# A value product issued one core step after its exponential, where it was issued two steps after

## The chip, the cores and the metric

The kernel runs on one core of a Trainium2 chip, as one launch. The metric is the device time of that launch in microseconds. Engines are named as in the profile: PE (TensorE matmuls), PEld (its weight loads), DVE (VectorE), ACT (ScalarE), POOL (GpSimd), SP (SyncE, which here only issues DMAs).

## What is computed

The input is a batch of 8 sequences of 1024 tokens with 256 channels, in float32. Each goes through six residual blocks, each on a layer norm: a gated feed-forward, a chunked linear attention, the feed-forward again, a routed low-rank expert block, a causal softmax attention, and the expert block again. The change is in the softmax attention:

```python
# 16 heads of 16 channels, scale = 16 ** -0.5; q and k carry a rotary embedding
scores = jnp.einsum('bhqd,bhkd->bhqk', q, k) * scale
scores = jnp.where(causal, -jnp.inf, scores)
attn = jax.nn.softmax(scores, axis=-1)
out = jnp.einsum('bhqk,bhkd->bhqd', attn, v)
```

## The kernel before, in words

**Three streams.** A front (feed-forward, linear attention, feed-forward, expert block, projections to q, k and v), a core (the softmax attention) and a tail (output projection and last expert block) run at the same time for different sequences. Each engine executes one fixed list of instructions, written by `weave` (L446). It counts ticks; in four of five ticks there is one core step `t`, and it calls the engine's core function three times, with `part` 0, 1 and 2. Between these calls come the pieces of the front for the first 512 tokens (after part 0), of the front for the last 512 tokens (after part 1) and of the tail (after part 2). No engine leaves its order.

**The core.** A group `g` is four heads of one sequence, 32 groups in all. A first pass computes scores (`score`, L730, with a mask added by a small matmul L733) whose row maxima DVE takes (`reduce_max`, L1083); the banks of these scores are a ring of two, shared with two kinds of transposes (L783, L789), so each score waits until DVE has read the one two places back. The maxima go back through DRAM as extra rows of the stacked q (`stq`), so that the second pass gets scores with the maximum already subtracted.

**The second pass** is cut into units `u`, 24 for a group and 768 in all: a half `c` of the queries, a block `kb` of 128 keys, and a pair `hp` of heads; even units hold heads 0 and 1 of the group and odd ones heads 2 and 3. Core step `t` has `u = t - SX`. In it

- PE computes the transposed scores of unit `u + 1` (`tscore`, L747), a matmul for each of two heads, into banks 0 and 1. The matmul of head `j` waits until ACT has read that bank for unit `u`.
- ACT takes the exponentials of unit `u` (L1283), one instruction a head, into `pexp`, a ring of `NPX = 4` units in SBUF. Before it writes slot `u % 4` it waits for `pv_done`, which counts value products of pairs.
- POOL sets the part over the diagonal to zero in units of the causal diagonal (`affine_select`, L1431; 16 of 24 units), one step after ACT in its own list.
- PE multiplies values and exponentials of a pair of units, four heads at once (`values`, L766; eight matmul records), into bank 2. It waits for the exponentials of the odd unit, for POOL's selects, and at the first key block of a half for ACT's copy of bank 2 (`ypv`, L1289) from the half before.
- When a half is complete ACT copies bank 2, PE transposes the copy (L783) and DVE divides by the row sums (L1070, L1074).

SP loads stacked q and k of a later group when the transposed scores of an earlier one are done (L1483), and rows of v when value products have let go of them (L1492).

The wait of ACT that matters below is this one:

```python
if u >= NPX:
    nc.scalar.wait_ge(s["pv_done"], (u - NPX) // 2 + 1)
```

For even `u` it asks for the pair whose last unit is `u - 3`; for odd `u` for the pair whose last unit is `u - 4`, which is the same pair. In the list of PE the kernel before issues the pair ending in unit `u - 2` at odd `u`, in part 1, so the pair that ends in `u - 3` comes right behind the transposed scores of the even unit `u`.

Of the kernel before, what the change touches and what calls it, by code (L numbers as in the profile page):

```python
# [18 lines left out]
NB = B  # L19
# [36 lines left out]
def macaron(nc, a, out):  # L56
    ctx = ExitStack()
    with ctx:
# [105 lines left out]
        def ps(i, n=1):  # L164
            return bank[i // 2][:, (i % 2) * CH:(i % 2) * CH + n * CH]
# [192 lines left out]
        NU = NTU * NG  # L358
# [23 lines left out]
        def width(c, kb):  # L382
            return CH - max(0, kb - 4 * c) * P
# [18 lines left out]
        if True:  # L402

            with nc.Block() as block:
# [22 lines left out]
                def r_take(*key):  # L427
                    n = len(rtab)
                    rtab[key] = n
                    if n >= 2:  # L430
                        nc.tensor.wait_ge(s["r_used"], n - 1)
                    return ps(3 + n % 2)
# [290 lines left out]
                def score(g, i):  # L723

                    h, qb, k0, k1 = sunits[i]
                    b_ = slot(g, h // 2)
                    nc.tensor.wait_ge(stack_in[b_], 16 * ND * loads(g, h // 2))
                    bk = r_take("s", g, i)
                    diag = k1 == P * (qb + 1)
                    last = mm(bk[:, 0:k1 - k0], stq[b_][:, h % 2, qb * P:(qb + 1) * P], stk[b_][:, h % 2, k0:k1],  # L730
                              start=True, stop=not diag)
                    if diag:
                        last = mm(bk[:, k1 - k0 - P:k1 - k0], identb[:], maskneg[:], start=False, stop=True)  # L733
                    last.then_inc(s["r_full"], 1)

                def tscore(u):

                    g, i = divmod(u, NTU)
                    c, kb, hp = tunits[i]
                    if i == 0:  # L740
                        nc.tensor.wait_ge(max_in[g % 2], 64 * (g // 2 + 1))
                    n = width(c, kb)
                    b_ = slot(g, hp)
                    for j in range(2):
                        if u >= 1:
                            nc.tensor.wait_ge(s["exp_done"], 2 * u + j - 1)
                        mm(ps(j)[:, 0:n], stk[b_][:, j, kb * P:(kb + 1) * P],  # L747
                                  stq[b_][:, j, (c + 1) * CH - n:(c + 1) * CH], start=True, stop=True).then_inc(
                                      s["t_ps"], 1)

                def values(u):

                    g, i = divmod(u, NTU)
                    c, kb, _ = tunits[i]
                    yu = NC * g + c
                    n = width(c, kb)
                    if g % NG == 0 and kb % 4 == 0:
                        nc.tensor.wait_ge(s["v_in"], 32 * (g // NG) + 16 * (kb // 4 + 1))
                    nc.tensor.wait_ge(s["exp_done"], 2 * u + 2)
                    if i in DIAG:  # L760
                        nc.tensor.wait_ge(s["causal"], len(DIAG) * g + DIAG.index(i) + 1)
                    if kb == 0 and yu >= 1:
                        nc.tensor.wait_ge(s["ypv_done"], yu)
                    for j in range(G):
                        at = VP * (G * (g % NG) + j)
                        last = mm(ps(2)[HP * j:HP * (j + 1), CH - n:CH], vsm[:, kb, at:at + HP], pexp[:, (u - 1 + j // 2) % NPX, j % 2, 0:n],  # L766
                                  start=kb == 0, stop=kb == 4 * c + 3, tile_position=(0, HP * j))
                    last.then_inc(s["pv_done"], 1)

                def core_pe(t, part):  # L770
                    u = t - SX
                    if part == 0 and 0 <= u + 1 < NU * NB:
                        tscore(u + 1)
                    if part == 1 and u % 2 and 3 <= u < NU * NB + 2:
                        values(u - 2)
                    if (t, part) in score_at:
                        score(*score_at[t, part])
                    if part == 2 and t in y_tr_at:
                        g, c = y_tr_at[t]
                        nc.tensor.wait_ge(s["ypv_done"], NC * g + c + 1)  # L780
                        bk = r_take("y", g, c)
                        for k in range(4):
                            last = nc.tensor.transpose(bk[:, k * P:(k + 1) * P], ypv[:, c, k * P:(k + 1) * P], ident[:])  # L783
                        last.then_inc(s["r_full"], 1)
                    if part == 2 and t in max_tr_at:
                        g = max_tr_at[t]
                        nc.tensor.wait_ge(s["mx_comb"], g + 1)
                        bk = r_take("m", g)
                        nc.tensor.transpose(bk[0:G * NT, 0:P], mxa[:, g % 2], ident[:]).then_inc(s["r_full"], 1)  # L789

                @block.tensor
                def _(pe):
                    weave(core_pe, front_pe, tail_pe)
# [782 lines left out]
```

## Time and profile before

| | |
|---|---|
| Median of three runs | 3236.56 us (3227.16 to 3240.71) |
| The profiled execution | 3248.06 us, span of the core 3246.3 us |
| PE busy | 2891.0 us, 89% of the span |
| DVE busy | 1852.1 us, 57% |
| ACT busy | 1215.9 us, 37% |
| POOL busy | 746.2 us, 23% |
| Granted TensorE clock over the span | 0.922 |
| First transposed score to the last value product | from 391.8 us to 3175.6 us |

The profile is of one execution. Busy time is the union of an engine's instructions; idle time before an instruction is put down to the engine and line whose semaphore ended it. Waits under 0.15 us are left out of the views of waits. The granted clock is 1.00 at 2.4 GHz and 0.5 at 1.2 GHz. A difference of less than about half a per cent can't be told from the spread of the runs.

### The profile page before, as it was taken

Reading aid. Unit: us, or ns where it says so; the run is one execution under the profiler, and the core shown is the slowest. Engines: PE = TensorE matmul, PEld = TensorE weight load, DVE = VectorE, ACT = ScalarE, POOL = GpSimd, SP = SyncE. Lnnn points to the kernel's source line nnn. Section 1 sums busy time; section 2 is a strip of 40 time slices with the busy share of each in tenths; the row PEclk is TensorE's granted clock in tenths of the full one; section 3 lists DMA queues with packets and bytes.
Section 4 is the critical chain, followed back from the end, with each engine's and each line's share of the span. In section 5 each row is a group of like instructions: output and inputs, shape, how many; then the busy total and the mean of one; then the engine's idle time right before and its main releaser. Section 6 shows DMA issues by size and latency. Waiting matters only on the chain.

```text
span 3246.3 us, 47003 instructions
## 1 busy us (share of the span) xinstructions
PE 2891.0 (89%) x16398; PEld 1811.0 (56%) x16398; DVE 1852.1 (57%) x4515; ACT 1215.9 (37%) x2706; POOL 746.2 (23%) x1276
## 2 busy tenths in 40 slices
PE   3885899899999998999999999999999999989987
PEld 2653565456656665556656566466555566555534
DVE  6443656655666556665566556565566655665532
ACT  1321244344334343443334343343434333343341
POOL 1321222222222222223222222222322222221110
PEclk7886899999999999999999999999999989999986
DMA  1024104311232204311333113322134113233101
GB/s 54 1 59 105 21 16 95 94 27 37 55 109 57 58 16 102 106 39 30 63 83 89 36 38 61 110 57 51 26 92 115 30 30 63 70 89 98 44 21 41
DMA packets 137424, 194.06 MB, mean 60 GB/s; under 512 B 49439, under 2 KB 111214, under 8 KB 127854
## 3 DMA queue, kind: packets, MB, share of 16 engines
q1 hardware_dynamic: 137198, 191.07, 23.9%
q8 instruction: 139, 2.28, 0.3%
q14 instruction: 87, 0.71, 0.1%
HBM read 122.34 MB, written 67.63 MB: 59 GB/s over the span
## 4 chain that ended last, share of the span: by engine, by line
PE 65%; DVE 12%; DMA 7%; ACT 4%; issue 3%; SPq 1%; POOL 1%; DVEq 0%; ACTq 0%; POOLq 0%
PE bank L747 9%; PE bank L730 8%; PE bank L766 8%; DMA stk<-k_halves 6%; PE bank L565 4%; PE bank L658 4%; PE bank L505 3%; PE bank L514 3%; PE bank L672 3%; PE bank L545 3%; ACT pexp L1283 3%; PE bank L496 2%; PE bank L659 2%; DVE mxa L1083 2%; PE bank L475 2%
## 5 line engine op out<-in xcount | busy, mean ns | idle before, releaser
L1283 ACT ACTIVATE pexp<-bank 128x512 f32<-128x512 f32 (+3 forms) x1536 | 675.1, 496 | 934.2 <-PE bank L766 748.2
L1083 DVE TENSOR_REDUCE mxa<-bank 128x1 f32<-128x512 f32 (+3 forms) x1024 | 595.3, 587 | 506.9 <-PE bank L733 296.9
L730 PE MATMUL bank<-stk,stq 128*128 128x512 f32 (+3 forms) x1536 | 604.0, 415 | 148.2 <-DVE mxa L1083 53.2
L747 PE MATMUL bank<-stq,stk 128*128 128x512 f32 (+3 forms) x1536 | 592.3, 444 | 73.9 <-ACT pexp L1283 66.5
L730 PEld LDWEIGHTS bank<-stk,stq 128*128 128x128 f32 x1536 | 300.6, 198 | 466.8 <-issue 408.3
L1431 POOL TENSOR_SCALAR_AFFINE_SELECT pexp<-pexp 128x256 f32<-128x256 f32 x512 | 217.1, 428 | 911.5 <-ACT pexp L1283 911.4
L747 PEld LDWEIGHTS bank<-stq,stk 128*128 128x128 f32 x1536 | 281.9, 198 | 253.8 <-ACT pexp L1283 181.5
L766 PE MATMUL bank<-pexp,vsm 128*32 128x512 f32 (+3 forms) x3072 | 345.1, 523 | 0.0
L1083 DVE TENSOR_REDUCE mxb<-bank 128x1 f32<-128x128 f32 (+3 forms) x512 | 248.0, 484 | 167.5 <-PE bank L733 165.2
L733 PE MATMUL bank<-maskneg,identb 128*128 128x128 bf16 x1024 | 243.4, 238 | 0.0
L1349 POOL TENSOR_SCALAR_AFFINE_SELECT arena<-arena 128x512 f32<-128x512 f32 x128 | 78.4, 636 | 438.9 <-ACT arena L1187 438.9
L565 PE MATMUL bank<-arena 32*128 32x256 f32 x1024 | 159.2, 431 | 14.8 <-DVE arena L893 11.1
L733 PEld LDWEIGHTS bank<-maskneg,identb 128*128 128x128 bf16 x1024 | 102.2, 100 | 123.6 <-issue 78.3
L475 PE MATMUL bank<-ident,arena 128*128 128x128 f32 x768 | 119.9, 307 | 38.9 <-DVE arena L810 38.7
L496 PE MATMUL bank<-arena,wk 128*128 128x256 f32 x512 | 144.4, 433 | 8.3 <-ACT arena L1187 4.6
L1300 POOL TENSOR_SCALAR varep<-mv 128x4 f32<-128x4 f32 x96 | 22.6, 235 | 542.6 <-DVE mv L804 541.8
L1104 ACT COPY xnT<-bank 128x512 f32<-128x512 f32 x160 | 89.3, 609 | 144.8 <-PE bank L475 144.2
L505 PE MATMUL bank<-wr,arena 128*128 128x256 f32 x512 | 132.8, 406 | 1.0
L1405 POOL TENSOR_TENSOR arena<-arena 128x1024 f32<-128x1024 f32 x32 | 75.9, 2372 | 246.7 <-DVE arena L1008 246.7
L893 DVE TENSOR_TENSOR arena<-bank,mask 128x512 f32<-128x512 f32 x128 | 82.3, 685 | 87.9 <-PE bank L565 87.9
L475 PEld LDWEIGHTS bank<-ident,arena 128*128 128x128 f32 x768 | 101.8, 163 | 48.4 <-DVE arena L810 41.6
L514 PE MATMUL bank<-wv,arena 128*128 128x256 f32 x512 | 122.0, 382 | 3.3 <-ACT arena L1191 3.2
(185 smaller groups left out, 4146.8 us busy)
## 6 DMA issues: line engine op xcount, KB each, us to landing
stq<-q_halves SPq DMA_DIRECT2D x128, 256.0 KB
arena<-rope_table SPq DMA_DIRECT2D x8, 2048.0 KB
q_halves<-arena SPq DMA_DIRECT2D x32, 512.0 KB, 2.9
k_halves<-arena SPq DMA_DIRECT2D x32, 512.0 KB, 2.8
stk<-k_halves SPq DMA_DIRECT2D x64, 256.0 KB
stk<-k_halves SPq DMA_DIRECT2D x128, 128.0 KB
v_rows<-arena SPq DMA_DIRECT2D x16, 544.0 KB, 4.1
vsm<-v_rows SPq DMA_DIRECT2D x16, 544.0 KB, 3.8
```

Source lines behind the costliest of these rows:

```text
L475: last = nc.tensor.transpose(bk[:, t * P:(t + 1) * P], src[:, t, k * P:(k + 1) * P], ident[:])
L496: last = mm(bk[:, m * D:(m + 1) * D], wk0[:, k, m * P:(m + 1) * P], xmA[:, h, k], start=k == 0, stop=k == KT - 1)
L505: last = mm(bk[:, i * D:(i + 1) * D], xmB[:, p, k, i * P:(i + 1) * P], wr0[:, k], start=k == 0, stop=k == KT - 1)
L514: last = mm(bk[:, i * D:(i + 1) * D], kact[:, p, k, i * P:(i + 1) * P], wv0[:, k], start=k == 0, stop=k == KT - 1)
L565: last = mm(bks[i][:, k * D:(k + 1) * D], khT[rows, k, j * P:(j + 1) * P], qbd[rows, j % 2, k], start=k == 0, stop=k == KT - 1, skip_group ...
L730: last = mm(bk[:, 0:k1 - k0], stq[b_][:, h % 2, qb * P:(qb + 1) * P], stk[b_][:, h % 2, k0:k1], start=True, stop=not diag)
L733: last = mm(bk[:, k1 - k0 - P:k1 - k0], identb[:], maskneg[:], start=False, stop=True)
L747: mm(ps(j)[:, 0:n], stk[b_][:, j, kb * P:(kb + 1) * P], stq[b_][:, j, (c + 1) * CH - n:(c + 1) * CH], start=True, stop=True).then_inc(s["t ...
L766: last = mm(ps(2)[HP * j:HP * (j + 1), CH - n:CH], vsm[:, kb, at:at + HP], pexp[:, (u - 1 + j // 2) % NPX, j % 2, 0:n], start=kb == 0, sto ...
L1083: nc.vector.reduce_max(dst, r_bank("s", g, i)[:, 0:k1 - k0], AX).then_inc(s["r_used"], 1)
L1283: nc.scalar.activation(pexp[:, u % NPX, j, 0:n], ps(j)[:, 0:n], ACT.Exp, scale=DK ** -0.5).then_inc(s["exp_done"], 1)
L1431: nc.gpsimd.affine_select(out=v, in_=v, compare_op=ALU.is_ge, fill=0.0, base=0, pattern=[[0, 2], [1, P]], channel_multiplier=-1).then_inc( ...
```

## The change

Value products are issued at even `u` in place of odd `u`, and of the pair that ends in `u - 1` in place of `u - 2`. Every value product moves one core step ahead in PE's list, still in part 1. Nothing else of any engine's list changes: the waits ask for the same counts, the ring has four slots as before, and the same instructions run with the same sizes.

```diff
@@ -771,8 +771,8 @@
                     u = t - SX
                     if part == 0 and 0 <= u + 1 < NU * NB:
                         tscore(u + 1)
-                    if part == 1 and u % 2 and 3 <= u < NU * NB + 2:
-                        values(u - 2)
+                    if part == 1 and u % 2 == 0 and 2 <= u < NU * NB + 1:
+                        values(u - 1)
                     if (t, part) in score_at:
                         score(*score_at[t, part])
                     if part == 2 and t in y_tr_at:
```

## Rows read from the trace of the kernel before

**Rows 1.** The page, busy time of PE (share of the span, instructions)

```profile
PE 2891.0 (89%) x16398; PEld 1811.0 (56%) x16398; DVE 1852.1 (57%) x4515; ACT 1215.9 (37%) x2706; POOL 746.2 (23%) x1276
```

**Rows 2.** The page, chain of work that ended last, by engine

```profile
PE 65%; DVE 12%; DMA 7%; ACT 4%; issue 3%; SPq 1%; POOL 1%; DVEq 0%; ACTq 0%; POOLq 0%
```

**Rows 3.** Windows: stretch, its length, busy time by engine, PEclk, DMA

```profile
392.00:3064.00 2672.00, 2471.52 (x14380) 1546.31 (x14380) 1598.07 (x3922) 1070.45 (x2399) 638.35 (x1088) 0.95 0.26 63
...
3129.00:3139.00 10.00, 8.18 (x34) 3.12 (x34) 0.00 (x0) 4.50 (x10) 1.63 (x4) 0.51 0.00 0
...
3157.00:3174.00 17.00, 12.98 (x64) 4.55 (x68) 0.00 (x0) 8.36 (x20) 2.85 (x7) 0.99 0.03 8
```

**Rows 4.** Waits of PE, 392 to 3176 us: total us, times, longest

```profile
PE bank L747 <- ACT pexp L1283: 66.5, 155, 1.0
PE bank L730 <- DVE mxa L1083: 47.3, 82, 1.6
PE bank L730 <- DVE mxb L1083: 27.6, 35, 2.0
PE bank L730 <- DMA stk<-k_halves: 22.1, 7, 4.0
```

**Rows 5.** Waits of ACT, whole span: total us, times, longest

```profile
ACT pexp L1283 <- PE bank L766: 748.2, 306, 8.8
```

**Rows 6.** Timeline: value product, exponential of an even unit, next transposed scores

```profile
2040.27 1.07 PE L766 MATMUL bank<-pexp,vsm 128*32 128x512 f32 x8
...
2041.40 1.09 ACT L1283 ACTIVATE pexp<-bank 128x512 f32<-128x512 f32 x2 [2.60 <-PE bank L766]
...
2042.05 0.99 PE L747 MATMUL bank<-stq,stk 128*128 128x512 f32 x2 [0.33 <-ACT pexp L1283]
```

**Rows 7.** Timeline: first and last of 89 such waits of odd units

```profile
492.41 0.99 PE L747 MATMUL bank<-stq,stk 128*128 128x512 f32 x2 [0.21 <-ACT pexp L1283]
...
3173.36 0.64 PE L747 MATMUL bank<-stq,stk 128*128 128x128 f32 x2 [0.40 <-ACT pexp L1283]
```

**Rows 8.** Timeline: an odd unit's wait behind front work of ACT

```profile
2207.96 1.33 ACT L1118 ACTIVATE arena<-xnT,mu 128x512 f32<-128x512 f32 x2
...
2209.20 1.07 ACT L1283 ACTIVATE pexp<-bank 128x512 f32<-128x512 f32 x2
...
2209.83 0.98 PE L747 MATMUL bank<-stq,stk 128*128 128x512 f32 x2 [1.01 <-ACT pexp L1283]
```

**Rows 9.** Timeline: first and last of 26 waits of that kind

```profile
430.55 0.98 PE L747 MATMUL bank<-stq,stk 128*128 128x512 f32 x2 [0.79 <-ACT pexp L1283]
...
2847.97 0.99 PE L747 MATMUL bank<-stq,stk 128*128 128x512 f32 x2 [0.40 <-ACT pexp L1283]
```

**Rows 10.** Timeline: first and last of 41 waits of even units

```profile
427.79 0.99 PE L747 MATMUL bank<-stq,stk 128*128 128x512 f32 x2 [0.66 <-ACT pexp L1283]
...
3171.58 0.60 PE L747 MATMUL bank<-stq,stk 128*128 128x128 f32 x2 [0.26 <-ACT pexp L1283]
```

**Rows 11.** Timeline of PE, one pair of units after the last score

```profile
3159.59 0.99 PE L747 MATMUL bank<-stq,stk 128*128 128x512 f32 x2 [0.72 <-ACT pexp L1283]
3160.84 0.98 PE L747 MATMUL bank<-stq,stk 128*128 128x512 f32 x2 [0.25 <-ACT pexp L1283]
3161.75 1.06 PE L766 MATMUL bank<-pexp,vsm 128*32 128x512 f32 x8
3163.53 0.98 PE L747 MATMUL bank<-stq,stk 128*128 128x512 f32 x2 [0.72 <-ACT pexp L1283]
```

**Rows 12.** Groups of instructions, 392 to 3176 us: busy us, mean ns

```profile
L1083 DVE TENSOR_REDUCE mxa<-bank 128x1 f32<-128x512 f32 x985 | 573.0, 587 | 481.3 <-PE bank L733 276.5 <-PE bank L730 200.8 <-DVE krs L866 0.2
L766 PE MATMUL bank<-pexp,vsm 128*32 128x512 f32 (+3 forms) x3072 | 345.1, 523 | 0.0
```

**Rows 13.** Timeline: a late select of POOL; ACT's copy of bank 2

```profile
494.43 1.19 POOL L1431 TENSOR_SCALAR_AFFINE_SELECT pexp<-pexp 128x256 f32<-128x256 f32 x3
...
3134.87 0.59 ACT L1289 COPY ypv<-bank 128x512 f32<-128x512 f32 x1
```

## The prediction

> **What bounds the kernel now.** I read the page's busy times first. PE is busy for 2891.0 of 3246.3 us, far more than any other engine [rows 1], and it carries 65% of the chain that ended last, where ACT has only 4% [rows 2]. So a change pays only by what it takes out of PE's idle time, or out of the clock. The windows say how much there is: from 392 to 3064 us, where all three streams run, PE is busy 2471.5 of 2672 us, so 200 us are idle, and the granted clock is 0.95 [rows 3].
>
> PE's waits say what ends that idle time. Transposed scores (L747) waited 66.5 us in 155 waits for an exponential; scores (L730) waited 47.3 and 27.6 us for DVE to empty the ring of two, and 22.1 us for a load [rows 4]. The change can act on the first directly.
>
> ACT's own waits name the cause of a part of them: 306 times an exponential waited for a value product, 748.2 us in all [rows 5]. Most of it is harmless, since ACT is busy 37% of the time. It harms where PE stands still for the exponential. At 2040.27 us a value product runs for 1.07 us, the exponential of the even unit starts right behind it, after 2.60 us of idling, and the transposed scores of the next, odd unit wait 0.33 us for it [rows 6].
>
> I sorted the waits of 0.15 us and more by what had held the exponential. Odd units behind a value product: 89, 28.0 us together [rows 7]. Odd units where ACT had been busy with front work: 26, 17.7 us, such as the 1.01 us at 2209.83, where front work (L1118) ran right up to the exponential [rows 8, 9]. Even units, whose exponential needs no new value product: 41, 21.8 us [rows 10]. That is 67.5 us, one wait more than the row of 66.5.
>
> **The change, part by part.** *The wait removed.* The exponential of an even unit asks for the pair that ends three units before. That pair now stands in PE's list one step earlier, ahead of the transposed scores that the exponential reads. The wait is met whenever those scores are there. The 89 waits behind a value product should go. Twelve of them, 6.8 us, lie after the last score (3121 us); 77, 21.2 us, before it.
>
> *The last stretch.* After 3121 us only transposed scores, exponentials and value products run. A pair of full width takes 3163.53 - 3159.59 = 3.94 us [rows 11]. In the new order the odd unit's 0.98 us are followed by the value product, 1.06 us, less the 0.1 us by which such blocks overlap in these rows, so the even unit starts 1.97 us after the odd one; and the next odd unit starts 1.25 us later, the same distance as 3160.84 - 3159.59, which is set by ACT. The sum is 3.2 us, 0.7 less. Some ten pairs, the last ones narrower: **7 us less**, all of it on the chain, as nothing else runs there.
>
> *The cover moved.* A value product is also work with which PE fills the time of an exponential: 345.1 us in 384 blocks is 0.90 us a block [rows 12]. It stood between the transposed scores of an even unit and of the next odd one, and will stand between those of an odd unit and the next even one. The even units' waits before 3121 us, 27 with 17.4 us, then lie behind 0.90 us more work, and nearly all (17 us) go. But the 26 waits behind front work of ACT stay where ACT puts them, while PE comes 0.90 us earlier: 26 times 0.90 is 23 us more. Bounds: none of it (if ACT, no longer held by value products, is through with its front work earlier) and 26 times 1.07, 28 us. I take 23, because in rows 8 ACT works without a gap up to the exponential. In full: -21.2 - 17 + 23 = -15 us of PE idle. Of that I count the 65% that PE has of the chain, since PE ahead of time within a stretch that DVE or a load sets gains nothing: **10 us less**.
>
> *The ring of two scores.* Each step has two scores. Where the value product leaves the space between them (odd steps) the second reaches PE's head 0.90 us sooner after the first; where it now stands (even steps), 0.90 us later. The waits for DVE come to 75 us in two rows [rows 4]. As many places gain cover as lose it, and the places that wait today mostly follow a step without a value product, which are those that gain. I take **5 us less**, with 25 us either way as bounds (a third of the 75).
>
> *New waits of the value product.* The exponentials of its odd unit are done, because the transposed scores of the next unit, ahead of it in the list, have already waited for them in both heads. POOL's select must be done as well, and had one step more before. Laid beside the new place (behind the transposed scores and the first score of that step), it would be late in 7 of 255 pairs, by 0.15 us each, all at the place of the row at 494.43, where three selects run together: **1 us more** [rows 13]. If POOL were late everywhere, by its 0.4 us a select, 255 times 0.4 would be 102 us; the rows exclude that, since 248 are in time. ACT's copy of bank 2, 0.59 us, comes just before the first value product of a half now [rows 13]; it starts as the exponential ends, when the second transposed score starts too, and a score follows. In none of 62 places would it be late: 0.
>
> *Moved past queues.* No DMA is issued with a value product. SP's loads of v wait for it (L1492) and can only start earlier. Scores, transposes and front matmuls between the old and the new place come up to 1.07 us later once, and the block is then behind them: no cost in sum.
>
> **The sum.** -7 - 10 - 5 + 1 = -21 us. The profiled execution took 3248.06 us (span 3246.3), 0.36% over the median of 3236.56; such a difference of 21 us is as good for the one as for the other. From the median: 3236.56 - 21, so **3215 us**, 0.7% less. About 0.5%, 16 us, is what a measurement of this kernel can tell from no change.
>
> The clock is the open term. From 3129 to 3139 us the granted clock was 0.51, the lower of its two levels with PE 82% busy; from 3157 to 3174 it was 0.99 with PE 76% busy [rows 3]. The Trainium skill, "TensorE: Matmul & The Clock Gate", Part 1 (The HAM clock gate), has it that idling takes the clock down and sustained work brings it up. Those two rows don't bear that out here, as the busier stretch is the slower; by the rule the 8.18 us of work in the first would take some 4 us less and the sum be -25.
>
> **The rivals.**
>
> *A: the waits move on (no change).* PE gets through the transposed scores earlier and meets the next wait: the ring, the load, or ACT's front work. For it: DVE's 75 us stand next to the 66.5, and 20% of the chain is DVE and DMA [rows 2, 4]. Against it: the last stretch has neither. It leaves the 7 us, and 3 or 4 of the core's: about 3227 us.
>
> *B: the full gain.* All 67 us of waits for exponentials go, since ACT, no longer held 748 us, does its front work ahead [rows 5], and 10 us of other waits with them; at 65% for the 56 us before 3121 plus those 10, and all of 11 after: 3236.56 - 43 - 11 = 3183 us. The Trainium skill, "Perfetto Trace Analysis" (Optimization Strategy), reads a gap that recurs on the engine to be saturated as a possible lack of buffers; by that rule freeing a slot of the ring earlier would close the whole of it. The trace agrees for 89 of the 156 waits; the 26 behind front work are against it.
>
> *C: slower, by the ring of two.* In 384 odd steps the second score now follows the first with no value product between. DVE needs 0.59 us on average for a row maximum [rows 12], two a step, so DVE front work that falls into such a step can put PE at a stand. An added wait of 0.2 us a step is 77 us, 50 at the chain's 65%: 3215 + 50 = 3265 us. It decides from 0.15 us a step on (58 us, 38 on the chain, which makes +16 of -21). Against it: the even steps gain the same cover.
>
> **How the numbers follow.** Forecast (3200 to 3230 us) 0.55; A 0.24; B 0.12; C 0.09. Of the forecast's own 0.55 I count 0.42 under 3220 us and 0.13 above. Faster: 0.42 + 0.12 + 0.03 of A = 0.57. Slower: C, 0.09. Same: 0.34. The range takes B's 3183 and most of A with the ring's bound of 25 us times 0.65 over 3215 to 3235, and a part of C: 3180 to 3243 us.
>
> **What would show it.** Right: ACT's wait for a value product falls from 748 us to under 100; L747's wait for exponentials falls to about 50 us, and what is left stands at odd units behind front work, the 1.01 us of rows 8 grown to about 2; no wait at L766 for POOL over 0.2 us; pairs in the last stretch of about 3.2 us. Wrong: waits of L730 for DVE (mxa and mxb) at 105 us or more (C, or A if the time stays); L766 waiting for L1431 or L1289; a granted clock that moved from 0.95 between 392 and 3064 us, where 0.01 is some 25 us of PE's 2471.

## The result and the profile after

The changed kernel takes 3126.31 us (median of four runs, 3122.58 to 3129.97) against 3237.75 us for the kernel before in the same comparison: a ratio of 0.9653, 95% interval 0.9633 to 0.9672. It is 111 us faster, where 21 were forecast, and lies outside the range of 3180 to 3243. The direction was right and the size was off by a factor of five.

The page of the changed kernel, whose profiled execution took 3122.58 us: span, busy times by engine, and two of its costliest groups (busy us, mean ns, idle time before).

```profile
span 3120.8 us, 47003 instructions
...
PE 2796.0 (90%) x16398; PEld 1767.2 (57%) x16398; DVE 1847.0 (59%) x4515; ACT 1213.2 (39%) x2706; POOL 741.6 (24%) x1276
...
L747 PE MATMUL bank<-stq,stk 128*128 128x512 f32 (+3 forms) x1536 | 544.0, 426 | 53.3 <-ACT pexp L1283 49.2
...
L766 PE MATMUL bank<-pexp,vsm 128*32 128x512 f32 (+3 forms) x3072 | 347.9, 526 | 8.3 <-POOL pexp L1431 8.2
```

The first thing to see is where the 125.5 us of span went. PE's idle time fell from 3246.3 - 2891.0 = 355.3 us to 324.8 us, by 30.5 us. Its *busy* time fell by 95.0 us, with the same 16398 matmuls [rows 1]. A forecast that counts idle time can't see the larger part.

The waits of PE from the first transposed score to the last value product (total us, times, longest), and the first of the waits of ACT over the span:

```profile
PE bank L747 <- ACT pexp L1283: 49.2, 56, 2.2
PE bank L730 <- DVE mxa L1083: 40.3, 68, 2.2
PE bank L730 <- DMA stk<-k_halves: 24.9, 14, 2.4
PE bank L730 <- DVE mxb L1083: 13.3, 19, 1.7
PE bank L789 <- DVE mxa L1083: 9.4, 13, 2.9
PE bank L783 <- DVE mxa L1083: 9.1, 22, 1.7
PE bank L766 <- POOL pexp L1431: 8.2, 14, 0.9
```

```profile
ACT pexp L1283 <- PE bank L747: 628.0, 441, 7.7
```

The wait of ACT for a value product, 748.2 us before [rows 5], has no row any more: an exponential now waits only for its own scores. Idle time before L747 is 49.2 us in place of 66.5, scores wait 53.6 us for the row maxima in place of 74.9 [rows 4], and the two kinds of transposes that share the ring wait 18.5 us where they waited 2.1.

The clock: windows of the changed kernel (columns as in rows 3).

```profile
392.00:2950.00 2558.00, 2382.95 (x14312) 1502.66 (x14311) 1583.94 (x3899) 1060.94 (x2385) 632.19 (x1085) 0.96 0.27 66
2950.00:3050.00 100.00, 92.14 (x517) 43.95 (x516) 42.60 (x86) 56.72 (x127) 15.04 (x37) 0.97 0.16 35
```

From 0.95 to 0.96 while all streams run [rows 3], and over the whole span from 0.922 to 0.938 in the two profiled executions. Its four runs had 0.934 to 0.938.

**Where the time went, matmul by matmul.** I took the distance from each matmul's start to the next one's, in each execution, and compared it with the short distances (the lowest tenth or so) that the same two forms have at the upper clock in all the runs. What is over, at the lower clock up to as much again as the short distance, is counted as clock; the rest goes to the line that comes late. I call such a matmul late. The figures are estimates, worked from the records of starts and of the granted clock, and good for differences between kernels more than as absolute times. From the first transposed score to the last value product the time fell from 2783.8 to 2663.6 us, by 120 us: late transposed scores 73 us less, late scores 40 us less, clock 34 us less; late transposes of the ring 21 us more and late value products 7 us more; the remainder is 1 us. With the lowest tenth taken strictly as the short distance, the first three are 68, 40 and 34 us, so they hold to about 5 us. Of those 68 us, 46 stand ahead of the first head of a pair and 22 between its heads. The time at the lower clock fell from 295 to 201 us in that stretch. Of the 1534 transposed scores with a predecessor in their bank, 571 started within 75 ns of the end of the exponential that they waited for; after the change, 251.

### The profile page after: what moved, and what is told of

It is laid out like the page before. It is cut to its first block, busy times and chain, and to the rows that moved or that the text cites. A ratio compares the mean times of both kernels' runs of the same rounds, so it can differ in the third digit from the quotient of the medians.

```text
span 3120.8 us, 47003 instructions
## 1 busy us (share of the span) xinstructions
PE 2796.0 (90%) x16398; PEld 1767.2 (57%) x16398; DVE 1847.0 (59%) x4515; ACT 1213.2 (39%) x2706; POOL 741.6 (24%) x1276
## 4 chain that ended last, share of the span: by engine, by line
PE 64%; DVE 12%; DMA 9%; issue 3%; ACT 2%; POOL 1%; SPq 1%; DVEq 0%; ACTq 0%; POOLq 0%
PE bank L730 9%; PE bank L747 7%; PE bank L766 7%; DMA stk<-k_halves 7%; PE bank L565 4%; PE bank L658 4%; PE bank L545 3%; PE bank L505 3%; PE bank L672 3%; PE bank L514 3%; DVE mxa L1083 3%; PE bank L659 2%; PE bank L496 2%; PE bank L600 2%; PE bank L475 2%
## 5 line engine op out<-in xcount | busy, mean ns | idle before, releaser
L730 PE MATMUL bank<-stk,stq 128*128 128x512 f32 (+3 forms) x1536 | 620.3, 418 | 115.0 <-DVE mxa L1083 46.2
L747 PE MATMUL bank<-stq,stk 128*128 128x512 f32 (+3 forms) x1536 | 544.0, 426 | 53.3 <-ACT pexp L1283 49.2
L747 PEld LDWEIGHTS bank<-stq,stk 128*128 128x128 f32 x1536 | 268.3, 199 | 176.0 <-ACT pexp L1283 110.3
L766 PE MATMUL bank<-pexp,vsm 128*32 128x512 f32 (+3 forms) x3072 | 347.9, 526 | 8.3 <-POOL pexp L1431 8.2
L733 PE MATMUL bank<-maskneg,identb 128*128 128x128 bf16 x1024 | 241.6, 236 | 0.0
L733 PEld LDWEIGHTS bank<-maskneg,identb 128*128 128x128 bf16 x1024 | 101.3, 99 | 120.3 <-issue 78.3
L496 PE MATMUL bank<-arena,wk 128*128 128x256 f32 x512 | 137.3, 417 | 4.6 <-DVE arena L834 4.5
L1125 ACT ACTIVATE arena<-bank 128x512 f32<-128x512 f32 x64 | 38.2, 597 | 226.6 <-PE bank L496 226.6
L505 PE MATMUL bank<-wr,arena 128*128 128x256 f32 x512 | 125.4, 389 | 1.0
L766 PEld LDWEIGHTS bank<-pexp,vsm 128*32 128x32 f32 x3072 | 62.6, 110 | 109.1 <-issue 79.9
## 6 DMA issues: line engine op xcount, KB each, us to landing
v_rows<-arena SPq DMA_DIRECT2D x16, 544.0 KB, 4.1
vsm<-v_rows SPq DMA_DIRECT2D x16, 544.0 KB, 3.8
```

The lines of the kernel that those rows point to most:

```text
L496: last = mm(bk[:, m * D:(m + 1) * D], wk0[:, k, m * P:(m + 1) * P], xmA[:, h, k], start=k == 0, stop=k == KT - 1)
L505: last = mm(bk[:, i * D:(i + 1) * D], xmB[:, p, k, i * P:(i + 1) * P], wr0[:, k], start=k == 0, stop=k == KT - 1)
L747: mm(ps(j)[:, 0:n], stk[b_][:, j, kb * P:(kb + 1) * P], stq[b_][:, j, (c + 1) * CH - n:(c + 1) * CH], start=True, stop=True).then_inc(s["t ...
```

## The experiments

All comparisons are with runs of the kernel before on the same chip, so the times of one table row are best read by their ratio.

| run | edit in short | us | ratio, 95% interval |
|---|---|---|---|
| changed kernel | | 3126.31 | 0.9653, 0.9633 to 0.9672 |
| e1_ring5_lag2 | ring of five, products as before | 3196.73 | 0.9866, 0.9834 to 0.9898 |
| e2_ring4_lag2 | control for e1 | 3229.51 | 0.9983, 0.996 to 1.0005 |
| e3_wait_back | changed, exponential held by a score | 3218.07 | 0.9941, 0.9916 to 0.9967 |
| e4_ahead_of_t | product just ahead of L747, odd step | 3196.0 | 0.9864, 0.9826 to 0.9903 |
| e5_ring6_even_lag3 | ring of six, even steps, three behind | 3209.25 | 0.9912, 0.9883 to 0.9941 |
| e6_v_before_scores | changed, product ahead of both scores | 3156.89 | 0.9745, 0.9719 to 0.9771 |
| e7_short_max_lag2 | before, short row maxima | 3180.51 | 0.9825, 0.9793 to 0.9856 |
| e8_short_max_lag1 | changed, short row maxima | 3074.26 | 0.9491, 0.945 to 0.9532 |
| e9_even_lag3_copy | e5 with later copies of bank 2 | 3163.39 | 0.9786, 0.9753 to 0.982 |
| e10_half_ends_1 | half of the change | 3204.89 | 0.9903, 0.987 to 0.9935 |
| e11_half_ends_3 | the other half | 3175.53 | 0.9817, 0.9783 to 0.9851 |
| e12_v_part2 | changed, product behind both scores | 3189.03 | 0.9839, 0.9789 to 0.9889 |
| e13_both_lag2 | before, both heads wait for both exponentials | 3314.17 | 1.0261, 1.0229 to 1.0293 |
| e14_both_lag1 | changed, the same | 3153.35 | 0.9766, 0.9752 to 0.9781 |

**Is it the freed exponential, or the moved product?** e1 frees the exponential and leaves the product; e3 moves the product and holds the exponential.

e1_ring5_lag2 (e2_ring4_lag2 has the shared tiles and keeps four slots):

```diff
-NPX = 4
+NPX = 5
-        wr0, wk0, wv0, wq1, wk1, wv1, wf1 = (...)
+        wr0, wk0, wv0, wq1, wf1 = (...)
+        wk1 = wv1 = wq1
```

> The order of the kernel before, value products two steps behind, but the ring of exponentials has five slots in place of four, so the exponential of an even unit asks for a value product that stands three steps back. The room comes from letting the k and v projections use the q weights' tile (their weights are not the reference's; sizes and instructions are the same). Theory 'held exponential' (what paid is that the exponential no longer waits for a value product, wherever the product stands): at least 80% of the 111 us come with this, 3125 to 3150 us, ACT's idle time before L1283 put down to L766 near 0, transposed scores held by an exponential in about 250 of 1534 matmuls where it was 571. Rival 'moved cover' (what paid is that the value product fills the time of another exponential, and the steps are more even): 3200 to 3230 us. Rival 'clock': the time follows the granted clock, which stays near 0.922, and the gain is under 60 us.

> Control for the run with five slots: the kernel before with the k and v projections using the q weights' tile and nothing else changed. Both theories: within 0.3% of the kernel before, 3228 to 3247 us.

e3_wait_back, on the changed kernel:

```diff
                         if u >= NPX:
                             nc.scalar.wait_ge(s["pv_done"], (u - NPX) // 2 + 1)
+                        if u % 2 == 0 and (t - 1, 1) in score_at:
+                            nc.scalar.wait_ge(s["r_full"], rtab[("s", *score_at[t - 1, 1])] + 1)
```

> The changed kernel, value products one step behind, but the exponential of an even unit waits in addition for the second score of the step before, which stands in PE's list where the value product stood before. So the product is moved and the exponential is held as before. 'Held exponential': 3210 to 3250 us, transposed scores held in over 500 matmuls. 'Moved cover': 3125 to 3150 us.

The control stands within the noise (0.9983). Freeing the exponential alone gives 1.3%, some 43 us, not 80% of the gain; moving the product with the exponential held gives 0.6%, some 19 us; both together 3.5%. Neither theory holds by itself; some 50 us come only when both are done. The waits of PE in e1, 392 to 3176 us (its lines are three further on: L733 is the score, L750 the transposed score), show what becomes of the first half alone:

```profile
PE bank L733 <- DVE mxa L1086: 63.8, 91, 1.8
PE bank L750 <- ACT pexp L1286: 40.0, 71, 1.0
PE bank L733 <- DVE mxb L1086: 34.6, 47, 2.0
```

ACT is not quite free in e1. Where an exponential no longer waits for a value product, the copy of bank 2 does, which it did once, for 1.3 us, in the kernel before:

```profile
ACT ypv L1292 <- PE bank L769: 47.1, 35, 2.4
```

The idle time before transposed scores falls from 66.5 to 40.0 us, and the scores' waits for DVE rise from 74.9 to 98.4 us [rows 4]. That is rival A at work. In the accounting by distances, late transposed scores fall by 75 us in e1, as much as in the changed kernel, late scores rise by 24 us, and the clock gives 6 us where it gave 34. So the copy's wait hardly shows at the transposed scores.

In e3 the hold is back, and it is longer than before: 124.0 us of idle time before L747, where the kernel before has 66.5 and the changed kernel 49.2.

```profile
PE bank L747 <- ACT pexp L1285: 124.0, 174, 2.2
PE bank L730 <- DVE mxa L1083: 24.2, 36, 1.1
PE bank L730 <- DVE mxb L1083: 11.6, 15, 1.7
```

So e3 is not the kernel before with another place for the product. The product no longer covers the held exponential, and late transposed scores rise by 39 us against the kernel before; in return late scores fall by 70 us. The moved product is worth more at the ring than the 19 us say, and the held exponential costs more than it did. The granted clock of its ten runs, 0.929 to 0.942, is that of the changed kernel.

**Does the place of the product count, with the exponential free?** e4, e6 and e12 have the changed kernel's freedom and other places.

```diff
 e4_ahead_of_t, on the kernel before
+                    if part == 0 and u % 2 and 3 <= u < NU * NB + 2:
+                        values(u - 2)
                     if part == 0 and 0 <= u + 1 < NU * NB:
                         tscore(u + 1)
-                    if part == 1 and u % 2 and 3 <= u < NU * NB + 2:
-                        values(u - 2)
```

> Value products still at odd u and of the pair ending two units before, but in part 0 ahead of the transposed scores of that step in place of part 1: moved by less than a step, just past L747 and the first score. The exponential of an even unit finds its slot free when its scores are there; POOL's select has nearly a step more time than in the changed kernel. 'Held exponential': as the changed kernel or a little better, 3115 to 3135 us, no wait of L766 for POOL. 'Moved cover': the product stands between the same two transposed scores as in the changed kernel, so the same, 3115 to 3135 us; it doesn't tell these two apart. If a full step of distance were what counted, under half of the gain: over 3180 us.

```diff
 e6_v_before_scores, on the changed kernel; e12_v_part2 has part == 2 there,
 behind the second score
-                    if part == 1 and u % 2 == 0 and 2 <= u < NU * NB + 1:
+                    if part == 0 and u % 2 == 0 and 2 <= u < NU * NB + 1:
                         values(u - 1)
```

> The changed kernel with the value product in part 0, directly behind the transposed scores and ahead of the first score of the even step, in place of between its two scores. Even steps keep the product; only its place between the scores goes. If the even length of steps is what relieves the ring of two: 3115 to 3150 us. If it is the place between the two scores: waits of the scores for DVE rise by 20 to 40 us and the time to 3150 to 3190 us. POOL's select has less time, so up to 10 us of waits of L766 for it.

> The changed kernel with the product one place further back, in part 2 of the even step, behind the second score and the front's work, ahead of the transposed scores of the next step. Exponentials are as free as in the changed kernel and POOL has more time. If the place between the two scores relieves the ring: 3140 to 3180 us, waits of the scores for DVE 20 to 40 us above those of the changed kernel. If not: within 15 us of 3126 us, or better by the 8 us that L766 waits for POOL.

Between the two scores of the even step it is 3126 us, ahead of both 3157, behind both 3189, and at the head of the next step 3196; the last two can't be told apart (their intervals overlap). In e12 the value product is issued behind one score and a piece of the front that it stood ahead of in the changed kernel, and that costs 63 us. So the expectation for e4, that neither theory gives more than 3135 us, was wrong, and with it the idea that the freed exponential and the same cover between transposed scores are all there is. Its time lies where a full step of distance was to have shown; but e12, with the distance of the changed kernel but for its place in the step, costs as much, so e4 doesn't show that. Not all of e6 is the ring: by distances, of 35 us between the profiled executions of e6 and the changed kernel, late value products (which wait for POOL, see below) are 25 us, the clock 20 and late scores 13, and late transposed scores are 12 us less. e12's waits, 392 to 3176 us, and its window (busy PE, PEld, DVE, ACT, POOL, PEclk):

```profile
PE bank L730 <- DVE mxb L1083: 50.3, 57, 2.0
PE bank L747 <- ACT pexp L1283: 47.2, 60, 2.2
PE bank L730 <- DVE mxa L1083: 38.6, 75, 2.2
```

```profile
392.00:2950.00 2558.00, 2361.63 (x13926) 1488.86 (x13924) 1528.89 (x3780) 1034.74 (x2319) 619.89 (x1061) 0.94 0.26 64
```

The wait for exponentials is the same as in the changed kernel (47.2 and 49.2 us). The scores wait 88.9 us for DVE where they waited 53.6, 35 more, as expected if the place relieves the ring (the time is 9 us over the range given for that), and the clock over that window is 0.94 where it was 0.96. By distances, against the changed kernel: late scores 50 us more, clock 46 us more, late transposed scores 11 us and late value products 7 us less, of 77 us in that stretch between the two profiled executions.

**The step, apart from the distance.** e5 puts the product into even steps three units behind, with a ring of six (further projections share a tile for their weights).

```diff
-                    if part == 1 and u % 2 and 3 <= u < NU * NB + 2:
-                        values(u - 2)
+                    if part == 1 and u % 2 == 0 and 4 <= u < NU * NB + 3:
+                        values(u - 3)
```

> Separates the step in which the value product stands from its distance to the exponential. The ring has six slots, so no exponential waits for a value product; the product is issued at even u as in the changed kernel, but of the pair that ends three units before (room for the ring: some projections share a tile for their weights, so their weights are not the reference's; instructions and sizes are the same). Against it stands the run with five slots and products at odd u, 3196.7 us. Theory 'two causes' (freed exponentials about -42 us alone; the product taken out of the long odd steps into the short even ones, between their two scores, gives the rest): 3115 to 3145 us, waits of the scores for DVE well under 100 us. Rival 'distance' (one step behind is what counts, for instance through the read of exponentials or the copies of bank 2): 3180 to 3210 us.

It took 3209 us, which would have spoken for the rival. But ACT's waits show a stall that the edit itself made, since the copy of bank 2 asked for a product of its own step:

```profile
ACT ypv L1293 <- PE bank L770: 184.2, 64, 6.1
```

So this run decides nothing by itself. e9 moves the copies and the transposes behind them (`sums_at`, `y_tr_at`) one core step later.

> The run with a ring of six and products at even u, three units behind, took 3209 us, but ACT stood 184 us before its copies of bank 2, which asked for a product of the same step; that hides what the place of the product does. Here the copies and the transposes behind them come one core step later, so ACT does not stand there. Theory 'two causes' (freed exponentials, and the product out of the odd steps into the even ones): 3120 to 3150 us, no wait of ACT's copy for L766, waits of L747 for exponentials near the 49 us of the changed kernel. Rival 'distance': 3180 us or more though ACT does not stand at the copy.

It took 3163 us. The copy's wait is shorter, but it is not gone, and two of PE's waits are above those of the changed kernel (the copy over the whole span, PE from 392 to 3176 us; L734 is the score, L751 the transposed score):

```profile
ACT ypv L1293 <- PE bank L770: 39.1, 40, 2.3
```

```profile
PE bank L751 <- ACT pexp L1287: 67.9, 76, 2.2
PE bank L734 <- DVE mxa L1087: 56.4, 73, 2.2
...
PE bank L734 <- DVE mxb L1087: 17.1, 14, 1.6
PE bank L734 <- DVE yst L1078: 14.3, 29, 1.2
```

By ratios e9 is some 26 us under e1, which has the product in odd steps, and 43 us over the changed kernel (33 and 37 us by medians). Neither range of the expectation was met. As far as the two can be compared, even steps help at a greater distance too, by roughly a third to a half of what e1 leaves. The rest is not shown to be distance. e9 also moves the transposes of the ring by a step, and 14.3 us of the scores' waits are for the division behind them, a row that the changed kernel lacks; ACT's copy still waits; and the further shared tiles of e5 and e9 have no control of their own. The clock of its four runs, 0.933 to 0.941, is not below that of the changed kernel, so it doesn't account for the difference.

**The halves.**

```diff
 e10_half_ends_1; e11_half_ends_3 has u % 4 == 0 and u % 4 == 3
-                    if part == 1 and u % 2 and 3 <= u < NU * NB + 2:
+                    if part == 1 and u % 4 == 2 and 2 <= u < NU * NB + 1:
+                        values(u - 1)
+                    if part == 1 and u % 4 == 1 and 3 <= u < NU * NB + 2:
                         values(u - 2)
```

> Half of the change: only pairs whose last unit is 1 modulo 4 come one step ahead; their product leaves the odd steps that are followed by a tick without a core step (5.30 us on average) for even steps of 2.72 us. The others stay two steps behind. If the two halves act by themselves and equally, 3170 to 3190 us. If the long steps matter more than the short ones, this half is worth 70 us or more: under 3167 us.

> The other half alone: pairs whose last unit is 3 modulo 4, whose product leaves odd steps of 3.88 us for even steps of 2.60 us. Equal halves: 3170 to 3190 us, and the two halves' gains sum to 100 to 120 us. If only the balance of all four steps pays, each half gives under 35 us and the sum falls short of 111.

They gain 1.0% and 1.8% (25 and 54 us), together 2.8% of the 3.5%, so the last 30 us need both, and e10 missed its range. The long step was not the better one to leave: the greater half is the one whose product leaves the step of 3.88 us. The halves also act in different places. By distances e10 has late transposed scores 29 us and late scores 28 us less than the kernel before; e11 has late transposed scores 59 us less and late scores 10 us more. Why the short step gains more at the transposed scores was not tested; that no tick of front work follows it, to cover the held exponential, would fit.

**The ring of two.** e7 and e8 shorten the row maxima in both orders; this leaves out part of the computation.

```diff
-                        nc.vector.reduce_max(dst, r_bank("s", g, i)[:, 0:k1 - k0], AX)
+                        nc.vector.reduce_max(dst, r_bank("s", g, i)[:, 0:P], AX)
```

> The kernel before, but each row maximum reads only the first 128 columns of its score, so DVE frees the ring of two sooner (the maxima are not those of the reference). Theory 'two causes': the ring is a cost of its own, so this gives 30 to 70 us by itself, 3170 to 3210 us. If the ring does not matter while exponentials are held: within 15 us of before.

> The changed kernel with the same short row maxima. 'Two causes': with the ring nearly free in both, the change is worth less than its 111 us: 50 to 85 us under the short-maximum kernel with products two steps behind, so 3100 to 3130 us. If the ring had no part in the gain, the difference stays at 100 to 115 us. Clock as a cause of its own: the difference stays in part even so, with the granted clock 0.01 or more above that of the other.

The ring costs by itself: 1.75%, some 56 us, in the kernel before. But the change is worth 106 us with short maxima too, not 50 to 85. The length of the maxima is not what the product's place relieves. By distances late scores still fall by 45 us between e7 and e8. That a score also waits because DVE has front work ahead of the maximum in its fixed order would fit; no run here tests it.

**Is the rest hidden in busy time?** In the rows a pair of transposed scores of 512 columns takes 0.99 us when held and 0.73 us when free. I read it so: the second head waits for its own exponential while the first still counts as busy. e13 and e14 let both heads wait for both exponentials, so that the whole hold stands ahead of the pair.

```diff
-                            nc.tensor.wait_ge(s["exp_done"], 2 * u + j - 1)
+                            nc.tensor.wait_ge(s["exp_done"], 2 * u)
```

> The kernel before, but the transposed scores of both heads wait until both exponentials of the unit before are done; so far each head waits for its own. The second head is then never held behind the first, and the whole hold stands ahead of the pair. If holds inside the pair are hidden in busy time: the idle time of L747 put down to the exponential rises from 66.5 us to 150 us or more, the busy time of L747 falls by 30 us or more (held pairs of 512 columns from 0.99 to about 0.75 us), and the time rises by 20 to 80 us. If the busy rows of L747 hold no wait: its busy time stays within 10 us of 592 us.

> The changed kernel with the same edit. Far fewer pairs are held (251 matmuls where it was 571), so there is less to move: the idle time of L747 rises by under half of what it rises in the other, its busy time falls by under 20 us, and the time rises by 5 to 40 us over 3126 us. The difference between the two orders then shows in the row of idle time itself: more than 60 us, where it was 17.

The group of the transposed scores on the page of the kernel before, then of e13 and of e14:

```profile
L747 PE MATMUL bank<-stq,stk 128*128 128x512 f32 (+3 forms) x1536 | 592.3, 444 | 73.9 <-ACT pexp L1283 66.5
```

```profile
L747 PE MATMUL bank<-stq,stk 128*128 128x512 f32 (+3 forms) x1536 | 533.8, 430 | 196.7 <-ACT pexp L1283 163.8
```

```profile
L747 PE MATMUL bank<-stq,stk 128*128 128x512 f32 (+3 forms) x1536 | 521.6, 422 | 101.0 <-ACT pexp L1283 95.2
```

In the kernel before 592.3 - 533.8 = 58.5 us of the busy time of L747 were holds, in the changed one 544.0 - 521.6 = 22.4 us (under 20 were expected). The wait inside a pair is shown. The clock doesn't explain the shorter busy time: it is lower in e13 and e14 (0.916 and 0.930 in the profiled executions) than in the kernels they are made from (0.922 and 0.938). The hidden holds of the two orders differ by 58.5 - 22.4 = 36 us; with the 66.5 - 49.2 = 17.3 us of visible ones that is 53 us. In e13 and e14 themselves the idle time differs by 163.8 - 95.2 = 68.6 us. That figure is too large as a measure, since the edit also adds holds: the first head now waits longer than it did, and idle time rises by 97.3 us in e13 where busy time falls by 58.5. e13 was dearer than expected (87 us over the kernel before, 20 to 80 expected), e14 within it (27 us, or 37 by ratios, 5 to 40 expected).

## Why the prediction was wrong in size

*The wait removed: right.* ACT's row for L766 is gone. *Front work of ACT: right.* The step of rows 8, in the changed kernel, where a front copy and L1118 hold ACT as before and PE comes earlier:

```profile
2138.01 1.33 ACT L1118 ACTIVATE arena<-xnT,mu 128x512 f32<-128x512 f32 x2
...
2139.25 1.07 ACT L1283 ACTIVATE pexp<-bank 128x512 f32<-128x512 f32 x2
...
2139.88 1.28 PE L747 MATMUL bank<-stq,stk 128*128 128x512 f32 x2 [2.20 <-ACT pexp L1283]
```

1.01 us became 2.20, and I had written about 2. The 56 waits that are left, 49.2 us, are near the 50 forecast.

*The last stretch: the pair right, the sum too small.* One pair of units after the last score, to be read against rows 11:

```profile
3040.05 0.99 PE L747 MATMUL bank<-stq,stk 128*128 128x512 f32 x2 [0.52 <-ACT pexp L1283]
3040.98 1.06 PE L766 MATMUL bank<-pexp,vsm 128*32 128x512 f32 x8
3041.97 0.73 PE L747 MATMUL bank<-stq,stk 128*128 128x512 f32 x2
3043.22 0.98 PE L747 MATMUL bank<-stq,stk 128*128 128x512 f32 x2 [0.51 <-ACT pexp L1283]
```

3043.22 - 3040.05 = 3.17 us, forecast 3.2. But the stretch from the last score (3120.7 us before, 3011.8 after) to the last value product went from 54.9 to 41.1 us, 14 us less in place of 7. Part of it ran at a clock of 0.51 before [rows 3], where my pair of rows 11 is from a part at 0.99: 26 us of that stretch were at the lower clock before and 7 after, which by distances is 5 of the missing 7 us.

*The cover moved: the step that failed.* I "sorted the waits of 0.15 us and more" and made the sum from them. That took idle time before an instruction for the time that PE is held. A held pair also loses 0.25 us between its heads, inside busy time. And behind a short matmul the last 0.19 us of its record count as busy while PE may already stand: the small matmul L733 lasts 0.23 us in the rows, and a free transposed score starts 0.04 us after its start, as here in the kernel before.

```profile
1504.53 0.23 PE L733 MATMUL bank<-maskneg,identb 128*128 128x128 bf16 x1
1504.57 0.48 PE L747 MATMUL bank<-stq,stk 128*128 128x256 f32 x2
```

Holds under 0.15 us were not in the sum at all. The idle time itself was forecast nearly right: 15 us less before 3121 us and at most the 6.8 us of waits behind it, against 17.3 us measured in all. Late transposed scores fell by 73 us in all: idle time was the wrong measure, not wrongly counted.

*The 65% of the chain: wrong too.* PE's matmuls lie in one fixed order, so the time of the stretch is the sum of their distances by arithmetic, and a hold that goes is gone unless another line comes later. That other line must be looked for and priced; e1 shows it, 24 us at the ring. A factor from the chain's shares stood in its place.

*The ring of two: sign right, size too small.* 5 us were forecast, within 25; by distances late scores fell by 40 us. The ring's transposes rose by 21, where "no cost in sum" was written. e12 and e4, and e6 in part, show that the place between the two scores of an even step matters. "As many places gain cover as lose it" was no argument, since steps are not alike. Before, the mean distances from one pair of transposed scores to the next, by `u % 4` from 0, were 2.60, 3.88, 2.72 and 5.30 us; after, 3.41, 2.67, 3.58 and 4.23.

*POOL: too small.* 8.2 us in 14 waits, 1 us forecast; with the product still earlier, in e6, it is 20.1 us. I had counted only lateness against instructions as they then stood in time, not with PE coming sooner.

*The clock: named as the open term, taken as zero.* By distances it gave 34 us. There is a second reading. The kernel before ran 40 times beside these experiments, between 3224.3 us at a granted clock of 0.930 and 3252.7 us at 0.924, and a straight line through the 40 gives 2.4 us for each 0.001 (correlation -0.85). From its median clock, about 0.927, to the changed kernel's 0.936 that is some 22 us. Both are estimates, from records and from a correlation that doesn't tell which of the two follows the other; no run here sets the clock. The Trainium skill, "TensorE: Matmul & The Clock Gate", Part 1, ties the clock to how busy PE has been. The trace agrees in sign for the changed kernel, which idles 30.5 us less and has the higher clock, and for e13, which idles more and has 0.916. It doesn't carry e12: PE is busy 89% of the span there, as in the kernel before, and the clock of its runs is 0.915 to 0.926 where that of the kernel before is 0.921 to 0.932. Nor does it carry e3, where PE is busy for less of the span, 88%, and the clock is the higher one, 0.929 to 0.942.

*The rivals.* A (the wait moves on) is what e1 did; in the changed kernel it is a small part, the 16 us more at the transposes and the 8.2 us at POOL. B was too small as well: it too was made from idle time. C did not come: the scores' waits for DVE fell.

What stays open: what takes the clock up or down (the product stands between the two scores of an even step in the changed kernel, e3 and e9, all at 0.929 or more, but also in e5, at 0.916 to 0.922); by what path the place relieves the scores; and why e9, in the same step, is some 40 us slower than the changed kernel. No version here that does all the work beats the changed kernel; e8, which is faster, leaves out work.

## What to carry to other kernels

On an engine whose instructions lie in a fixed order, size a hold by the distance from start to start against the shortest such distance of the same two forms, and not by the idle time before it: here 17 us of idle time stood for some 70 us. Then ask which wait comes next, and put the moved work where that one is relieved as well; freeing the exponential gave 1.3%, and freeing it with the work between the two scores of an even step 3.5%. Where a hold may hide inside a group, one run that moves the whole wait ahead of the group makes it visible in the fall of the group's busy time; the rise of idle time overstates it. And when one wait of an engine is taken away, look for the next wait of that same engine, as at ACT's copy in e1, e5 and e9, before the run is read as a clean test.

## What the runs showed of the hardware

- Two matmuls of 128x512 (f32 in the rows) to two banks take 0.73 us in the records from the first's start to the second's end when free, and 0.98 to 0.99 us when the second waits for an exponential; the whole counts as busy. The Trainium skill, "Trainium Kernel Development and Optimization" (Performance Expectations), calls matmul busy time a bad metric for how close a kernel is to its limit, because matmuls are pipelined. The trace agrees that it is no measure of work: 95 us of it went with not one matmul fewer, by less holding and by the clock.
- The granted clock differed with the order of the same 16398 matmuls: runs at 0.934 to 0.938 with the product between the scores (changed kernel), 0.925 to 0.932 ahead of them (e6), 0.915 to 0.926 behind them (e12), 0.914 to 0.918 at the head of the next step (e4). It did not go by PE's busy share in the profiled execution: runs at 0.929 to 0.942 with a share of 88% (e3), at 0.915 to 0.926 with 89% (e12).
- Within one kernel the time goes with the clock: 40 runs of the kernel before, 2.4 us less for each 0.001 more, with a correlation of -0.85.
